# Attention: the product of probabilities and values in three fp32r passes, with the steps of all engines in a new order

## The reference

```
q, k, v = x @ Wq.T, x @ Wk.T, x @ Wv.T          # 16 heads of 128
scores  = q @ k.T / sqrt(128)
scores  = clip(scores, -1024, 1024)
scores  = scores + slope[head] * key_position, -inf where key > query
attn    = softmax(scores)
z       = attn @ v
out     = z @ Wo
```

## Time and profile before

| | |
|---|---|
| median of three runs | 1826.97 us |
| the profiled execution | 1828.67 us, its span 1826.9 us |
| mean granted TensorE clock | 0.977 of full speed |
| attention stage | about 0 to 1007 us of the span |
| one pair of heads in it | 60.4 us |

### The profile page before, as it was taken

One profiled execution on the slowest core, in us unless ns is written; L12 is line 12 of the kernel. 1 busy time (PEld: TensorE's weight loads), 2 busy tenths in 40 slices (PEclk: granted clock), 3 DMA queues, 4 the chain that ended last, 5 costly groups with the idle time before them and its releaser, 6 DMA issues. The chain is left out here.

```text
span 1826.9 us, 29555 instructions
## 1 busy us (share of the span) xinstructions
PE 1698.9 (93%) x9152; PEld 1309.2 (72%) x9152; DVE 1385.8 (76%) x2105; ACT 1133.9 (62%) x2120; POOL 632.1 (35%) x507
## 2 busy tenths in 40 slices
PE   5999999999999999999999898879899899897998
PEld 4777787778787878778877787656457655456887
DVE  6777777777777777777775665888888788886996
ACT  3555655565556555555555553799996899883442
POOL 2332333232323232323221111049784089690000
PEclk9999999999999999999999998989999999998999
DMA  2000000000000000000000100023220122140000
GB/s 94 18 30 18 23 17 29 17 23 17 27 15 24 16 25 14 23 25 15 15 6 1 48 0 1 3 81 104 81 92 12 38 92 103 70 138 1 1 24 24
DMA packets 25088, 64.12 MB, mean 35 GB/s; under 512 B 2816, under 2 KB 8960, under 8 KB 24768
## 3 DMA queue, kind: packets, MB, share of 16 engines
q1 hardware_dynamic: 25024, 63.31, 10.5%
HBM read 60.94 MB, written 2.36 MB: 35 GB/s over the span
## 5 line engine op out<-in xcount | busy, mean ns | idle before, releaser
L2024 POOL TENSOR_SCALAR prob<-prob,rinv 128x640 f32<-128x640 f32 (+7 forms) x256 | 213.5, 835 | 674.3 <-DVE rinv L1423 673.2
L2100 POOL TENSOR_TENSOR m_h<-m_h,m_C 128x1024 f32<-128x1024 f32 x128 | 305.8, 2393 | 193.7 <-DVE m_h L1902 193.4
L1902 DVE TENSOR_TENSOR_SCAN m_h<-m_y,ps 128x1024 f32<-128x1024 f32 x128 | 291.5, 2284 | 52.7 <-PE ps L841 48.2
L968 ACT ACTIVATE prob<-prob,nmax 128x640 f32<-128x640 f32 (+7 forms) x256 | 198.3, 774 | 192.6 <-DVE nmax L1417 192.5
L526 PE MATMUL ps<-pt,v_sb 128*128 128x512 f32 (+3 forms) x768 | 310.3, 486 | 1.9 <-ACT pt L975 1.7
L975 ACT ACTIVATE pt<-ps 128x512 f32<-128x512 f32 (+3 forms) x384 | 186.0, 484 | 151.3 <-PE ps L516 150.1
L848 PE MATMUL ps<-m_h,ident 128*128 128x512 f32 x512 | 250.2, 612 | 11.3 <-POOL m_h L2100 11.3
L1417 DVE CUSTOM_DVE_ANT_0 prob<-prob,bias 128x640 f32<-128x640 f32 (+7 forms) x256 | 204.6, 799 | 44.9 <-issue 27.6
L516 PEld LDWEIGHTS ps<-ident,prob 128*128 128x128 f32 x1152 | 145.6, 140 | 116.6 <-issue 87.5
L1412 DVE TENSOR_SCALAR prob<-ps 128x640 f32<-128x640 f32 (+7 forms) x256 | 192.4, 752 | 42.3 <-PE ps L497 40.4
L1289 ACT ACTIVATE m_u<-m_uT,m_bT 128x256 f32<-128x256 f32 x512 | 210.6, 495 | 8.6 <-PE ps L841 8.6
(11 more groups left out here) (227 smaller groups left out, 3471.9 us busy)
## 6 DMA issues: line engine op xcount, KB each, us to landing
m_C<-bc_dram SPq DMA_DIRECT2D x64, 512.0 KB, 3.6
wqk_raw<-wqk_in SPq DMA_DIRECT2D x16, 512.0 KB, 3.2
wv_raw<-wv_in SPq DMA_DIRECT2D x16, 256.0 KB, 2.6
wo_raw<-wo_in SPq DMA_DIRECT2D x16, 256.0 KB, 2.9
x<-x_in SPq DMA_DIRECT2D x2, 1024.0 KB, 6.8
q_raw<-wgu_in SPq DMA_DIRECT2D x8, 256.0 KB, 2.8
raw<-wgu_in SPq DMA_DIRECT2D x1, 2048.0 KB, 8.4
out<-x SPq DMA_DIRECT2D x8, 256.0 KB, 2.2
```

The lines of the kernel that those rows point to most:

```text
L968: nc.scalar.activation(prob[:, at:at + n], prob[:, at:at + n], ACT.Exp, bias=nmax[:, k:k + 1], scale=-1.0, accum_out=rsum[:, k:k + 1]).the ...
L1902: nc.vector.tensor_tensor_scan(m_h[:, 2 * (v % 2) + e, :], m_da[:, 2 * (v % 2) + e, :], drive(e), 0.0, ALU.mult, ALU.add).then_inc(scan_do ...
L2024: nc.gpsimd.tensor_scalar(prob[:, at:at + n], prob[:, at:at + n], rinv[:, k:k + 1], 1.0, ALU.mult, ALU.mult).then_inc(norm_done, 1)
L2100: nc.gpsimd.tensor_tensor(state, state, m_C[:, v, :], ALU.mult).then_inc(hc_done, 1)
```

## The change

1. **Product in three passes.** `v_sb` becomes `v_hi` and `v_lo`, `pt` becomes `pt_hi` and `pt_lo`, all fp32r. ACT writes the hi parts, DVE the lo parts from PSUM less hi (`v_rest`, `pt_rest`). `pe_product` has three matmuls; the third waits for the lo part of `pt`. The 128-column block is widened to 256 columns with a half that is zero (`edge_hi`, `edge_lo`).
2. **Clip.** ACT copies a row's scores from PSUM to `prob` (`copy`), which frees the banks; POOL clips them there (`clip`); DVE only masks (`mask`).
3. **Weights.** The lo parts of Wv and Wo move from POOL to DVE (`v_weights_rest`, `out_weights_rest`), with a semaphore of their own for Wv.
4. **Order.** The table `USES` and the bodies of ACT, DVE and POOL are written anew; rows are loaded, masked and exponentiated in three different orders (`LOAD_ROWS`, `MASK_ROWS`, `EXP_ROWS`). The prologue loads row 6 first.

```diff
-        ROWS = (4, 5, 0, 1, 2, 3, 6, 7)
-        USES = ("v1", "s12", "s13", "out1", "s8", "qk0", "s9", "s10", "s11", "qk1", "s14", "s15",
-                "qk2", "s4", "s5", "qk3", "s0", "s1", "s2", "s3", "s6", "v0", "s7", "out0")
+        LOAD_ROWS = (6, 4, 5, 0, 1, 2, 3, 7, 12, 13, 8, 9, 10, 11, 14, 15)
+        MASK_ROWS = (4, 5, 0, 1, 2, 3, 6, 7, 12, 13, 8, 9, 10, 11, 14, 15)
+        EXP_ROWS = (0, 1, 2, 3, 4, 5, 6, 7, 12, 13, 8, 9, 10, 11, 14, 15)
+        USES = ("s12", "v1", "s13", "out1", "s8", "s9", "s10", "s11", "qk0", "s14", "qk1", "s15",
+                "qk2", "s6", "s4", "qk3", "s5", "s0", "s1", "s2", "s3", "v0", "s7", "out0")
         HALF = len(USES) // 2
         FIRST_S = 12
...
             if prev == -2:
-                pe.wait_ge(s_read, p * 20 + FIRST_S)
+                pe.wait_ge(s_copied, p * 16 + 8)
             elif prev == -1 and begin:
                 pe.wait_ge(v_read, 1)
             elif prev == -1:
                 pe.wait_ge(o_added, p * 2 - 1)
-            elif USES[prev][0] in "qs":
-                pe.wait_ge(s_read, s_count(p, USES[prev], last))
+            elif USES[prev][0] == "q":
+                pe.wait_ge(s_read, p * 4 + (4 + int(USES[prev][2:]) + 1))
+            elif USES[prev][0] == "s":
+                pe.wait_ge(s_copied, copy_count(p, USES[prev], last))
...
+        def turned(tiles, edge, idx, r0):
+
+            return edge[:, P:2 * P] if r0 == 3 else tiles[:, idx % 2, r0 * P:BANK]
...
             u, g, j, r0 = value_block(idx)
-            pe.wait_ge(pt_read, p * 24 + (idx + 1 + 2))
+            c0 = min(r0, 2) * P
+            pe.wait_ge(pt_split, p * 24 + (idx + 1))
             if j == 0:
                 pe.wait_ge(z_read, p * 4 + (2 * u + g + 1))
             if u == 0 and j % 4 == 0:
                 pe.wait_ge(v_read, p * 2 + (j // 4 + 1))
-            nc.tensor.matmul(ps[:, 6 + g, r0 * P:BANK], v_sb[:, j, u * DH:(u + 1) * DH],
-                             pt[:, idx % 2, r0 * P:BANK], start=(j == 0),
-                             stop=(j == 4 * g + 3)).then_inc(pv_done, 1)
+            for i, (a, w) in enumerate(((0, 0), (0, 1), (1, 0))):
+                if a:
+                    pe.wait_ge(pt_read, p * 24 + (idx + 1 + 2))
+                cols = (edge_hi, edge_lo)[a][:, :] if r0 == 3 else (pt_hi, pt_lo)[a][:, idx % 2, c0:BANK]
+                mm = nc.tensor.matmul(ps[:, 6 + g, c0:BANK], (v_hi, v_lo)[w][:, j, u * DH:(u + 1) * DH], cols,
+                                      start=(j == 0 and i == 0), stop=(j == 4 * g + 3 and i == 2))
+            mm.then_inc(pv_done, 1)
...
+            def copy(p, k, count, pos):
+                at, n = causal_row(k)
+                o = score_cols(k % 8)[0]
+                act.wait_ge(s_full, count)
+                flat = ps[:, s_bank(pos):s_bank(pos) + 2, :].rearrange("p a n -> p (a n)")
+                nc.scalar.activation(prob[:, at:at + n], flat[:, o:o + n], ACT.Copy).then_inc(s_copied, 1)
...
-            def scores(p, k, count, pos):
+            def mask(p, k):
                 at, n = causal_row(k)
-                o = score_cols(k % 8)[0]
                 tile = prob[:, at:at + n]
-                dve.wait_ge(s_full, count)
-                flat = ps[:, s_bank(pos):s_bank(pos) + 2, :].rearrange("p a n -> p (a n)")
-                nc.vector.tensor_scalar(tile, flat[:, o:o + n], CLIP, -CLIP, ALU.min, ALU.max).then_inc(s_read, 1)
                 dve.wait_ge(bias_ready, p * 2 + (k // 8 + 1))
-                dve.wait_ge(s_read, count)
+                dve.wait_ge(s_clipped, row_count(p, k, LOAD_ROWS))
                 dve.sem_inc(seen, 1)
 
                 nc.vector.tensor_tensor_reduce(out=tile, in0=tile, in1=bias[:, k // 8, S - n:S], scale=-1.0,
                                                scalar=BIG, op0=ALU.add, op1=ALU.min,
                                                accum_out=nmax[:, k:k + 1]).then_inc(masked, 1)
 
+            def pt_rest(p, idx):
+                r0 = value_block(idx)[3]
+                dve.wait_ge(pt_split, p * 24 + (idx + 1))
+                nc.vector.tensor_tensor(turned(pt_lo, edge_lo, idx, r0), ps[:, 4 + idx % 2, r0 * P:BANK],
+                                        turned(pt_hi, edge_hi, idx, r0).bitcast(F32),
+                                        ALU.subtract).then_inc(pt_read, 1)
...
+            def clip(p, k):
+                at, n = causal_row(k)
+                pool.wait_ge(s_copied, row_count(p, k, LOAD_ROWS))
+                pool.sem_inc(seen, 1)
+                nc.gpsimd.tensor_scalar(prob[:, at:at + n], prob[:, at:at + n], CLIP, -CLIP,
+                                        ALU.min, ALU.max).then_inc(s_clipped, 1)
```

More of the change, by code:

```diff
@@ L313, in s_count, with copy_count, row_count @@
             return p * 20 + (FIRST_S + len(mine))
-        def row_count(p, k):
-            return p * 16 + (8 * (k // 8) + ROWS.index(k % 8) + 1)
+        def copy_count(p, name, last=False):
+            mine = [n for n in USES[:USES.index(name) + 1] if n[0] == "s" and has(n, False, last)]
+            return p * 16 + (8 + len(mine))
+        def row_count(p, k, order):
+            return p * 16 + (order.index(k) + 1)
         @block.sync
@@ L512, in pe_transposes @@
             if j == 0:
-                pe.wait_ge(norm_done, p * 16 + max(row_count(0, 8 * u + 4 * g + r) for r in range(4)))
+                pe.wait_ge(norm_done, p * 16 + max(row_count(0, 8 * u + 4 * g + r, EXP_ROWS) for r in range(4)))
             for r in range(r0, 4):
@@ L991, in next_exps, with own_copy, next_copy @@
                         exps(p + 1, k)
+                def own_copy(k):
+                    copy(p, k, s_count(p, f"s{k}", last), USES.index(f"s{k}"))
+                def next_copy(k):
+                    if not last:
+                        copy(p + 1, k, s_count(p, f"s{k}"), USES.index(f"s{k}"))
                 pts(p, 0)
-                v(p, 1, 0)
+                exps(p, 7)
+                own_copy(12)
                 pts(p, 1)
@@ L1495, in body, with next_mask @@
                 q_scales, q_signs, q_values = q_parts(p, b)
-                def own(k):
-                    scores(p, k, s_count(p, f"s{k}", last), USES.index(f"s{k}"))
-                def ahead(k):
+                def next_mask(k):
                     if not last:
-                        scores(p + 1, k, s_count(p, f"s{k}"), USES.index(f"s{k}"))
+                        mask(p + 1, k)
                 def next_recip(k):
@@ L1515, in body @@
                     z_rest(p - 1, 1, 1)
-                own(12)
-                own(13)
-                recip(p, 12)
+                if not last:
+                    head_bias(p + 1, nb, 0)
+                v_rest(p, 1, USES.index("v1"))
+                pt_rest(p, 2)
+                mask(p, 12)
+                pt_rest(p, 3)
+                mask(p, 13)
+                q_scales()
                 if not begin:
                     residual(p - 1, before, 1, USES.index("out1"))
+                pt_rest(p, 4)
@@ L1521, in body @@
+                recip(p, 12)
+                pt_rest(p, 5)
                 recip(p, 13)
-                own(8)
-                q_scales()
+                pt_rest(p, 6)
                 z_rest(p, 0, 0)
+                mask(p, 8)
+                pt_rest(p, 7)
+                mask(p, 9)
+                pt_rest(p, 8)
+                mask(p, 10)
+                mask(p, 11)
+                if not last:
+                    v_weights_rest(p + 1)
                 recip(p, 8)
                 next_qk(0)
-                own(9)
@@ L1541, in body @@
-                next_qk(2)
-                z_rest(p, 0, 1)
-                ahead(4)
-                ahead(5)
+                next_qk(1)
+                pt_rest(p, 11)
+                pt_rest(p, 12)
+                recip(p, 14)
+                out_weights_rest(p)
+                mask(p, 15)
+                next_qk(2)
+                pt_rest(p, 13)
+                pt_rest(p, 14)
+                z_rest(p, 0, 1)
+                recip(p, 15)
+                pt_rest(p, 15)
+                q_values()
@@ L1580, in dve_attention @@
             qk(0, 3, 3)
-            for i, k in enumerate(ROWS):
-                scores(0, k, 5 + i, i if i < 7 else 8)
-                if i:
-                    recip(0, ROWS[i - 1])
-                if i == 3:
-                    dve_norm_lo(dve, 1, a_xl[1], a_xh[1], 4)
+            v_weights_rest(0)
+            for k in MASK_ROWS[:4]:
+                mask(0, k)
+            dve_norm_lo(dve, 1, a_xl[1], a_xh[1], 4)
+            mask(0, 2)
+            recip(0, 0)
+            mask(0, 3)
+            recip(0, 1)
+            mask(0, 6)
+            v_rest(0, 0, 7)
+            recip(0, 2)
+            recip(0, 3)
+            mask(0, 7)
+            recip(0, 4)
             body(0, 0, 0, begin=True)
```

271 lines of the change are left out of this document (171 added, 100 removed).

## The result

Before: 1827.63 us (median of four, 1826.77 to 1829.5). After: 1808.36 us (median of four, 1806.79 to 1810.54). The ratio is 0.9894, 95% interval 0.988 to 0.9907. The change makes the kernel faster, by 19.3 us; the forecast was 40.

What follows compares the result with a forecast made beforehand. PE was taken to bound each 60.4 us pair; less 2.2 (products) and 1.5 (old waits), plus 1.2 (new waits), 57.9. Fifteen pairs at 2.5 less, prologue 5 less, last pair 2 more: 1787 us, range 1768 to 1819.

Steps and rivals of the forecast that it cites:

- PE's products: Attention products as three fp32r passes instead of one fp32 instruction: net gain of 2.2 us a pair on PE.
- PE's old waits: PE's waits for projection rests on DVE, 1.5 us a pair, which the new order can remove entirely.
- Floor: Time of a pair of heads without new waits: 60.4 - 2.2 - 1.5 = 56.7 us.
- New waits: PE waiting for banks that DVE frees late at slots 3, 5, 12 and 1: 1.2 us a pair, 0 to 3.
- The places: Slots 3, 5, 12 and the next pair's 1, where PE wants a bank DVE frees late: 0.4, 0.2, 0.2, 0.4 us.
- rival 3: Eight masks wait, or two of four places cost a us each: 58.9 to 60.1 a pair, 1802 to 1819; chance 0.15.
- disturbed by POOL: A DVE instruction that finds POOL at work waits for its end; this set the upper ends at the four slots.
- Other engines: Busy time a pair forecast at DVE 50.3 us, ACT 44.6, POOL 29.2; none reaches 56.7, so PE still bounds.
- Prologue: Before the first pair, DVE loses seven clips and their pauses: 5 us gained, 1 to 7.
- Last pair: No projections fill PE and each row's chain is longer with clips on ACT plus POOL: 2 us lost, 0 to 4.
- 2 (DVE bound by POOL): Each of 16 masks waits for a POOL instruction, making DVE the bound: 62 us a pair, 1846 us; chance 0.10.
- 4 (the three passes gain nothing): Weight loads or transposes eat the passes' gain, only old waits go: 58.9 to 60.1 a pair, 1802 to 1819; chance 0.06.

Runs made afterwards that it cites:

- e6: The changed kernel with the product as one fp32 instruction as before, without low parts of the probabilities and values: 1810.3 us.
- e5: The changed kernel with each POOL clip cut to the first 8 columns of its row, the rest left unclipped: 1775.0 us.
- e4: The changed kernel with POOL's clip of row 7 of the next pair ahead of the normalizations of rows 2 and 3: 1810.1 us.
- e13: The changed kernel with q/k weights' low part on DVE, residual addition before mask 7, projection 1's rest before signs, v's cast earlier, scales and bias moved: 1783.9 us.
- e1: The changed kernel with DVE's residual addition (p, 0), which frees slot 1's banks, ahead of mask 7 of the next pair: 1840.8 us.

## Why the prediction was half right

- **PE's products**, 2.2 us a pair: right in each size (0.70, 0.52, 0.35). Between two fully fed kernels, e6 and e5, it is 2.2 in the first entry and 2.0 in the second. Transposes behind three passes cost nothing to be seen (four take 0.36 us at 180.31).
- **PE's old waits**, 1.5: right; e6, which has them removed and nothing added, takes 58.9 in the second entry and 59.2 in the first.
- **Floor**, 56.7: after less its waits gives 56.8, e5 56.9 to 57.0.
- **New waits, 1.2 us a pair: the step that failed.** The places were right but for slot 3, which had none; the sizes were not. Forecast for slots 3, 5, 12 and 1: 0.4, 0.2, 0.2, 0.4. Measured in the first entry: 0, 0.46, 0.79, 1.12, and 0.23 at slot 17; in the second 0, 0.19, 0.25, 1.13. 2.6 and 1.6 us, so that pairs took 59.4 and 58.4 instead of 57.9. From the start of pair 1 to that of pair 15 PE gained 21.8 us and not 14 x 2.5 = 35: 13.2 of the 18.6 us that the profiled execution came out above its forecast. It is rival 3 ("half of that") in its time and its mechanism: two of the four places cost about a us each in the first entry, one in the second, and the mean pair is 58.9.
- **Why they were too small.** I took masks "disturbed by POOL" as one interval's upper end, with each of POOL's instructions at its length in before. At slot 1 the trace shows three things: the clip starts late behind normalizations (166.81), it takes 1.35 us where it meets DVE's bias instruction (166.18, 1.09 us) instead of the 1.04 it takes alone in the same trace, and the mask behind it is held by the next POOL instruction as well (1.77 instead of 1.22). e5 keeps the first and the third and has a clip of 0.51, and the wait falls from 1.12 to 0.17; e4 takes the clip ahead of two normalizations, and slot 1 waits no more. The prediction ended a held mask with POOL's instruction, since a mask of 128 columns did so within 0.13 us; that one takes 0.29 alone, and a mask of 1024 columns ends 1.07 behind it. I had also taken away 2.8 us of DVE's idle time ahead of the masks; it stayed.
- **Other engines.** DVE 47.1 and 45.7 us a pair (forecast 50.3, 48 to 50), ACT 42.9 (44.6), POOL 30.7 (29.2). The sums were close and decide little: e13 runs at 57.1 to 57.6 with more on DVE, 48.5.
- **Prologue**, 5 us: the first transposes begin 6.8 us earlier (47.70 for 54.49), but the first pair (pair 0), which should have gained 2.5, loses 1.4: it takes 61.3 instead of 59.9, with waits for POOL's normalizations and the copies behind them. Pair 1 starts at 108.96 instead of 114.36, 5.4 earlier where 7.5 was forecast.
- **Last pair**, 2 us of loss: from its start to the end of its output product it took 45.9 us before and 52.3 after, a loss of 6.4. A half clock on top of the waits, which I had not counted, is part of it: 0.51 from 964 to 968, while in before the clock stays at 1.00 from 960 to 1006.
- **Rivals.** 2 (DVE bound by POOL) didn't come true in after, though e1 shows its mechanism at 61.3 us a pair; by its own terms (1827 + 24 - 3) its time should read 1848 and not 1846. 4 (the three passes gain nothing) is half true for another reason than it gave: PE gains its 2.0 us, and the low parts give them back as waits.
- **The rule of the Trainium skill** that I weighed (SBUF — State Buffer, the practical consequences of the shared port pair) agrees with the runs in its direction: the mask, with two SBUF inputs, took 3.16 us beside POOL's long instruction, while in after, during that instruction, a low part from PSUM (171.19) took 0.67 and the residual addition (170.06) 1.21, their usual times.

Together: 1788.2 forecast for the profiled execution; 13.2 for pairs 1 to 14, 2.1 for the prologue with pair 0 and 4.4 for the last pair, less 1.0 by which the later stages came out shorter, make 1806.9, and it took 1806.8.

What stays open: why POOL's instructions last longer beside DVE's (held at their start, or slowed all along) was not tried apart, nor was a clip on ACT or DVE for row 7 alone, nor the old order with the clip on POOL.
